# A fused graph, state-space and expert kernel: mask products of the decay exponents replaced by spare contraction rows, and their packets regrouped

## The chip, the cores and the metric

The kernel runs on one core of a Trainium2 chip. The metric is the device time of one execution, in microseconds (us): the median of three timed runs before the change is 3523.06 us (3521.47 to 3528.71). The profile is of one further execution of 3495.61 us.

The engines are TensorE (PE, its weight loads PEld), VectorE (DVE), ScalarE (ACT), GpSimd (POOL) and SyncE (SP). Each has its own instruction stream; they are tied by semaphores.

## The reference, cut to what matters

64 graphs of 256 tokens and 256 features pass through attention over the graph's edges, a state-space block, a product with four kinds of relation, and experts. The change is in the state-space block:

```
dt    = softplus(dt + dt_bias);  A = -exp(A_log)        # 8 heads
dA    = dt * A;  cs = cumsum(dA)                        # per head, over 256 tokens
L     = exp(where(l >= s, cs[l] - cs[s], -inf))         # 8 x 256 x 256
xdt   = x * dt
Y     = einsum('ln,sn,hls,shp->lhp', C, B, L, xdt)      # state size 64, head size 64
```

After it come `Y + x*D`, a product with `silu(z)`, a norm and the output product. Attention (`softmax`, then `probabilities @ wh`) and the relation products belong to other graphs at the same moment, as told below.

## The kernel before, in words

**Steps.** The 64 graphs go through a software pipeline written out by hand. `step(b1_, b2_, b3_, turn_)` issues, on each engine, stage 1 (attention) of graph b1, stage 2 (state space) of graph b2 = b1 - 1 and stage 3 (relations, the row for the experts) of graph b3 = b1 - 2. `rounds` calls it 66 times: some steps written out, and a hardware loop of 28 rounds with two steps each. The order in each engine's stream is the order in the text; nothing reorders it. The two steps of a round differ: one makes the routing decisions of four token tiles (`best_expert`, `counts`; TensorE's small products L1197 to L1202) and is called the routing step here, the other turns them into slots (`slots`, VectorE's L907 to L918) and is called the slot step. The expert stage (71 tiles) follows after all steps.

**The exponents.** Per head the matrix `cs[l] - cs[s]` is made on TensorE in one PSUM bank: 256 columns for sources s in the first 128 tokens and 128 columns for those in the second. `cs3` holds `cs` in bf16 as three parts (high, middle, low), 8 heads each, in 24 rows; four copies of it lie at partitions 0, 32, 64 and 96. `expo(heads, b)` issues a packet: for each of its heads a mask product (L1219, identity times `negmask`, 256 columns, which puts -1e30 above the diagonal), then the products with `sel` (L1224, +cs[l]) and with `selneg` (L1229, -cs[s]), which contract over 24 rows at 32 times q, q = head mod 4. Before, there are two packets: heads 0 to 3 and heads 4 to 7. `EXPO` names the bank of q.

**The chain around them.** `g` is B C^T (in bank 5, with dt turned beside it); ScalarE copies it out (L728 of the listing, L630 in the profile, since the helper `copy` records it). VectorE makes `xdt` (L991). ScalarE takes the exponential of each head (L743) into `decay`, VectorE multiplies pairs of heads by `g` (`weigh`, L868), and TensorE makes Y (L1391). Between these lie, on TensorE: `relate` (L1191, the relation products), the turns of the attention probabilities (L1348), which ScalarE copies out as `probT` (L630), the product with `wh` (L1373), and `attend` (L1184), the next graph's first products. `attend` writes the banks from which VectorE reads for `x1` (L1016), so it waits for `x1_ready`. VectorE's order is: softmax's scores (`nmax`, L975), `xdt`, slots (in the slot step), `weigh` of heads 0 to 3, `x1`, its statistics, `weigh` of heads 4 to 7, y.

## Time and profile before

| | us |
|---|---|
| median of three timed runs | 3523.06 (3521.47 to 3528.71) |
| the profiled execution | 3495.61 |
| its span | 3493.5 |
| TensorE busy | 3387.3 (97%) |
| VectorE busy | 2481.1 (71%) |
| ScalarE busy | 1794.4 (51%) |
| GpSimd busy | 1812.4 (52%) |

The span is the time from the first to the last instruction of the profile; the profiled execution is 2.1 us longer. The busy time of TensorE counts the stretch from a product's start to its modelled end, and neighbouring products overlap, so starts tell more than durations. Where a row of the timeline has xN, its first number is the start of the first of N instructions.

### The profile page before, as it was taken

To read this page: it belongs to the slowest core of one execution; us is meant where nothing else is said; L and a number is where in the kernel's file an instruction comes from. 1 tells how busy PE (TensorE), PEld (TensorE's weight loads), DVE (VectorE), ACT (ScalarE), POOL (GpSimd) and SP (SyncE) were. 2 spreads that over 40 slices of the span, in tenths; PEclk is the share of its full clock that TensorE was granted. 3 is DMA by queue.
4 is the path that set the end of the run, shared out by engine and by line. 5 is a ranking of instruction groups with operands and counts; after the bars stand their busy time and mean duration, and the time that the engine had idled before them with its cause. 6 is when DMAs were issued, how large, how long until landed. Compare 5 with 4: busy or idle time off the path is not lost.

```text
span 3493.5 us, 62587 instructions
## 1 busy us (share of the span) xinstructions
PE 3387.3 (97%) x19338; PEld 2778.6 (80%) x19338; DVE 2481.1 (71%) x7221; ACT 1794.4 (51%) x3818; POOL 1812.4 (52%) x2172
## 2 busy tenths in 40 slices
PE   7999999999999999999999999997799999999998
PEld 6777777777777777777777777775688888888887
DVE  4888888888888888888888888886344444444444
ACT  3655666656656656656666566563232223333322
POOL 3455555555555555555555555554455445555543
PEclk8999999999999999999999999998899999999999
DMA  3111111111111111111111111110455555555553
GB/s 125 40 37 47 44 36 52 39 36 51 39 43 48 36 44 47 36 52 39 36 51 39 42 49 36 45 44 23 161 192 192 197 196 190 194 198 195 194 192 129
DMA packets 168166, 304.67 MB, mean 87 GB/s; under 512 B 38000, under 2 KB 140400, under 8 KB 149936
## 3 DMA queue, kind: packets, MB, share of 16 engines
q0 software_dynamic: 38272, 196.98, 16.4%
q1 hardware_dynamic: 92880, 72.41, 7.3%
q10 hardware_dynamic: 36960, 34.62, 3.4%
q8 instruction: 27, 0.44, 0.1%
q14 instruction: 27, 0.22, 0.0%
HBM read 250.77 MB, written 53.17 MB: 87 GB/s over the span
## 4 chain that ended last, share of the span: by engine, by line
PE 93%; issue 2%; DVE 2%; ACT 1%; another core or an unknown queue 1%; DMA 1%; POOL 0%; SPq 0%; DVEq 0%; ACTq 0%; POOLq 0%
PE bank L1175 15%; PE bank L1447 14%; PE bank L1461 14%; PE bank L1191 13%; PE bank L1292 7%; PE bank L1406 6%; PE bank L1391 5%; PE bank L1184 4%; PE bank L1373 3%; PE bank L1323 2%; PE bank L1245 2%; PE bank L1314 1%; PE bank L1219 1%; PE bank L1413 1%; DVE x L1016 1%
## 5 line engine op out<-in xcount | busy, mean ns | idle before, releaser
L779 ACT ACTIVATE decay<-bank,w_up 128x256 f32<-128x256 f32 x568 | 269.4, 474 | 699.6 <-PE bank L1447 699.6
L1175 PE MATMUL bank<-xn1T,w_in 128*128 128x256 f32 x2304 | 524.9, 382 | 8.0 <-issue 7.2
L1191 PE MATMUL bank<-w_rel,hT 128*128 128x264 f32 x2048 | 523.6, 394 | 0.0
L1447 PE MATMUL bank<-zs,w_up 128*128 128x256 f32 x2272 | 503.9, 380 | 0.6 <-ACT zs L630 0.6
L1461 PE MATMUL bank<-w_dn,decay 128*128 128x256 f32 x2272 | 502.1, 379 | 0.0
L1175 PEld LDWEIGHTS bank<-xn1T,w_in 128*128 128x128 f32 x2304 | 433.2, 190 | 67.0 <-issue 10.4
L1447 PEld LDWEIGHTS bank<-zs,w_up 128*128 128x128 f32 x2272 | 433.0, 191 | 60.1 <-issue 0.9
L1461 PEld LDWEIGHTS bank<-w_dn,decay 128*128 128x128 f32 x2272 | 426.2, 190 | 55.1
L1123 DVE TENSOR_TENSOR hT<-bank,w_dn 128x256 f32<-128x256 f32 x142 | 60.3, 425 | 539.0 <-PE bank L1461 539.0
L859 DVE SCALAR_TENSOR_TENSOR conv<-bank,conv_w,conv 128x255 f32<-128x255 f32 (+2 forms) x960 | 426.2, 477 | 20.9
L1191 PEld LDWEIGHTS bank<-w_rel,hT 128*128 128x128 f32 x2048 | 364.0, 190 | 80.0 <-issue 20.8
L499 POOL TENSOR_SCALAR masks<-adjt_sb 128x512 fp32r<-128x512 int32 x256 | 404.5, 1594 | 5.4
L485 POOL TENSOR_TENSOR rstd<-ve,mhalf 128x2 f32<-128x2 f32 x256 | 217.5, 850 | 279.9 <-DVE ve L844 236.0
L363 POOL TENSOR_TENSOR beats<-mhalf 128x1 f32<-128x1 f32 x372 | 82.4, 221 | 462.1 <-DVE hT L1123 338.7
L868 DVE TENSOR_TENSOR decay<-decay,g 128x768 f32<-128x768 f32 x256 | 251.8, 1025 | 88.7 <-ACT decay L743 86.2
L536 POOL TENSOR_TENSOR x2b<-x,b_rel 128x264 f32<-128x264 f32 x128 | 92.9, 746 | 409.7 <-DVE xdt L991 401.3
L1292 PE MATMUL bank<-masks,xp 128*128 128x512 f32 x1024 | 276.6, 414 | 5.6 <-ACT xp L630 5.6
L743 ACT ACTIVATE decay<-bank 128x384 f32<-128x384 f32 x512 | 209.8, 496 | 115.0 <-PE bank L1229 97.0
L1292 PEld LDWEIGHTS bank<-masks,xp 128*128 128x128 f32 x1024 | 189.5, 190 | 68.5 <-ACT hT L630 25.3
L1406 PE MATMUL bank<-w_proj,y 128*128 128x264 f32 x1024 | 239.1, 387 | 0.3 <-DVE y L1032 0.3
L1406 PEld LDWEIGHTS bank<-w_proj,y 128*128 128x128 f32 x1024 | 189.4, 190 | 30.4 <-DVE y L1032 1.4
L635 ACT ACTIVATE conv<-bank,conv_b,conv_w 128x256 f32<-128x256 f32 x320 | 165.7, 558 | 68.3 <-PE bank L1175 68.3
(242 smaller groups left out, 6063.3 us busy)
## 6 DMA issues: line engine op xcount, KB each, us to landing
token_rows<-row SPq DMA_DIRECT2D x64, 266.0 KB, 3.0
xT_sb<-in_xT ACTq DMA_DIRECT2D x64, 256.0 KB, 2.7
x_sb<-in_x ACTq DMA_DIRECT2D x64, 256.0 KB, 3.0
adj_sb<-in_adj SPq DMA_DIRECT2D x64, 256.0 KB, 3.4
adjt_sb<-in_adjT SPq DMA_DIRECT2D x64, 256.0 KB, 3.4
out<-row SPq DMA_DIRECT2D x64, 256.0 KB, 2.4
w_in<-token_rows,idc POOLq DMA_INDIRECT x142, 4.8
out<-hT,ids POOLq DMA_INDIRECT x142, 2.5
```

Of the source, the lines that this page charges most:

```text
L485: gp.tensor_tensor(rstd[i][:], ve[i][:], mhalf[:], ALU.pow).then_inc(rstd_ready[i], 1)
L499: ins = gp.tensor_scalar(masks[:, :, r, :], adjt[:], float(r + 1), None, ALU.is_equal)
L743: nc.scalar.activation(decay[:, h, :], bank[EXPO[h % 4]][:, 0:TRI], ACT.Exp).then_inc(decay_ready, 1)
L779: nc.scalar.activation(hid(f), bank[f % 4][:, 0:GROUP], ACT.Relu, bias=b1[q % 2][:, f:f + 1]).then_inc(hid_ready, 1)
L859: ins = v.scalar_tensor_tensor(conv[:, c, k:N], src[:, 0:N - k], conv_w[:, c, TAPS - 1 - k:TAPS - k], conv[:, c, k:N], ALU.mult, ALU.add)
L868: v.tensor_tensor(decay[:, 2 * j:2 * j + 2, :], decay[:, 2 * j:2 * j + 2, :], g[:, 0:TRI].unsqueeze(1).broadcast_to([P, 2, TRI]), ALU.mult ...
L1175: ins = mm(dst, w_in[:, k, first:first + P], xn1T[:, k, :], start=k == 0, stop=k == DK - 1)
L1191: ins = mm(bank[6 + t][:, 0:GX], hT[:, d, r * N + t * P:r * N + (t + 1) * P], w_rel[:, r, d, :], start=r == 0 and d == 0, stop=r == R - 1 ...
L1292: ins = mm(bank[6 + c][:, :], xp[part][:, t, d * P:(d + 1) * P], masks[:, t, 2 * c:2 * c + 2, :], start=t == 0 and part == 0, stop=t == T ...
L1406: ins = mm(bank[(4, 2)[t]][:, 0:GX], y[:, j, t * P:(t + 1) * P], w_proj[:, j, :], start=j == 0, stop=j == XB - 1)
L1447: ins = mm(bank[f % 4][:, 0:GROUP], w1[i][:, k, f * P:(f + 1) * P], xgT[:, k, :], start=k == 0, stop=k == DK - 1)
L1461: ins = mm(bank[4 + j][:, 0:D], hid(f)[:, j * P:(j + 1) * P], w2[i][:, f, :], start=f == 0, stop=f == FB - 1)
```

## The change

1. **Masks.** The mask products and `identb`, `negmask` are gone. The contraction now takes all 32 rows of a group. The 29 rows that the head does not use carry, in `cs3`, a function of the position that steps from a tiny value to one at one multiple of 4 each, and in `selneg` -2^60 for the sources in question, so that what lies far above the diagonal is masked by the same products. Rows are prepared once, in VectorE's start; `cs` still comes from one scan (its first operand is now `factors`, its start 1.0).
2. **What is left above the diagonal**, within 4 positions, is cut by `causal` (ones and zeros): VectorE multiplies bank 3 by it and writes `g` (in place of ScalarE's copy), and `weigh` takes min(decay, 1) before it multiplies.
3. **Banks.** `EXPO` is (2, 3, 4, 5), `g` is made in bank 3, x is turned in banks 4 and 5. All eight banks are one tensor, so that ScalarE takes the exponentials of two heads in one instruction of 768 elements.
4. **Packets.** There are three: heads 0 and 1 ahead of `relate(1, range(0, 2))`, heads 2 and 3 where heads 0 to 3 were, heads 4 to 7 where they were. ScalarE takes the exponentials of heads 0 and 1 between the probabilities and the copy `probT`.
5. ScalarE's two copies of 8 columns to `x` are one.

TensorE in a written-out step of all three stages, before, from the turns of x (L1323) to `attend`:

```order
L1323 MATMUL bank<-identf,xs 128x128 x8
L1191 MATMUL bank<-w_rel,hT 128x264 x4
L1348 MATMUL bank<-identf,prob 128x128 x4
L1219 MATMUL bank<-negmask,identb 128x2x128 x4
L1224 MATMUL bank<-cs,sel 128x256 x4
L1224 MATMUL bank<-cs,sel 128x128 x4
L1229 MATMUL bank<-selneg,cs 128x256 x4
L1229 MATMUL bank<-selneg,cs 128x128 x4
L1373 MATMUL bank<-wh,probT 128x264 x4
L1219 MATMUL bank<-negmask,identb 128x2x128 x4
L1224 MATMUL bank<-cs,sel 128x256 x4
```

The same place in the changed kernel (`relate` is L1230 there, the turns of the probabilities L1389, the product with `wh` L1414):

```order
L1362 MATMUL bank<-identf,xs 128x128 x8
L1259 MATMUL bank<-cs,sel 128x256 x2
L1263 MATMUL bank<-cs,sel 128x128 x2
L1268 MATMUL bank<-selneg,cs 128x256 x2
L1268 MATMUL bank<-selneg,cs 128x128 x2
L1230 MATMUL bank<-w_rel,hT 128x264 x4
L1389 MATMUL bank<-identf,prob 128x128 x4
L1259 MATMUL bank<-cs,sel 128x256 x2
L1263 MATMUL bank<-cs,sel 128x128 x2
L1268 MATMUL bank<-selneg,cs 128x256 x2
L1268 MATMUL bank<-selneg,cs 128x128 x2
L1414 MATMUL bank<-wh,probT 128x264 x4
```

The rows of the masks are gone, a packet of two heads stands right behind the turns of x, and a packet of two heads, in place of one of four with its masks, stands between the turns of the probabilities and the product that reads `probT`.

VectorE in the same step, before, from the scores to `x1`:

```order
L975 TENSOR_SCALAR nmax<-emax 128x2
L991 TENSOR_TENSOR xdt<-bank,g 128x512 x2
L868 TENSOR_TENSOR decay<-decay,g 128x768 x2
L1002 RECIPROCAL rsum<-esum 128x2
L1016 SCALAR_TENSOR_TENSOR x<-bank,rsum,x_sb 128x264 x2
```

And in the changed kernel:

```order
L1012 TENSOR_SCALAR nmax<-emax 128x2
L1026 TENSOR_TENSOR g<-bank,causal 128x400
L1030 TENSOR_TENSOR xdt<-bank,g 128x512 x2
L904 SCALAR_TENSOR_TENSOR decay<-decay,g 128x768 x2
L1041 RECIPROCAL rsum<-esum 128x2
L1055 SCALAR_TENSOR_TENSOR x<-bank,rsum,x_sb 128x264 x2
```

The product that makes `g` is new in VectorE's stream, between the scores and `xdt`.

The diff, cut to its core:

```diff
-    EXPO = (2, 5, 3, 4)
+    EXPO = (2, 3, 4, 5)
...
+            def exponentials(j, b):
+                act.wait_ge(expo_made, 8 * b + 2 * j + 2)
+                if j == 0:
+                    need(act, y_made, 2 * b)
+                nc.scalar.activation(decay[:, 2 * j:2 * j + 2, :], expo_banks[j % 2][:, :, 0:TRI],
+                                     ACT.Exp).then_inc(decay_ready, 1)
...
                 nc.scalar.preload_act_table(ACT.Exp)
-                if b2_ is not None:
-                    act.wait_ge(g_made, b2_ + 1)
-                    need(act, m_ready, 4 * b2_)
-                    copy(g[:], bank[5][:, 0:TRI + T * H]).then_inc(g_ready, 1)
...
+                if b2_ is not None:
+                    exponentials(0, b2_)
+                if b1_ is not None:
                     act.wait_ge(prob_turned, b1_ + 1)
                     need(act, hp_made, b1_)
                     copy(probT[:], bank[0][:, :]).then_inc(probT_ready, 1)
                 if b2_ is not None:
-                    for h in range(H):
...
+                    for j in range(1, H // 2):
+                        exponentials(j, b2_)
...
                 for j in pairs:
-                    dve.wait_ge(decay_ready, 8 * b + 2 * j + 2)
-                    v.tensor_tensor(decay[:, 2 * j:2 * j + 2, :], decay[:, 2 * j:2 * j + 2, :],
-                                    g[:, 0:TRI].unsqueeze(1).broadcast_to([P, 2, TRI]), ALU.mult).then_inc(m_ready, 1)
+                    dve.wait_ge(decay_ready, 4 * b + j + 1)
+                    v.scalar_tensor_tensor(decay[:, 2 * j:2 * j + 2, :], decay[:, 2 * j:2 * j + 2, :], 1.0,
+                                           g[:, 0:TRI].unsqueeze(1).broadcast_to([P, 2, TRI]), ALU.min,
+                                           ALU.mult).then_inc(m_ready, 1)
...
-                    ch2.link(dve, v.tensor_tensor_scan(cs[:], ones_row[:], dA[:], 0.0, ALU.mult, ALU.add), b2_)
+                    ch2.link(dve, v.tensor_tensor_scan(cs[:], factors[:], dA[:], 1.0, ALU.mult, ALU.add), b2_)
...
                 if b2_ is not None:
+                    dve.wait_ge(g_made, b2_ + 1)
+                    v.tensor_tensor(g[:], bank[3][:, 0:GW], causal[:], ALU.mult).then_inc(g_ready, 1)
                     dve.wait_ge(g_ready, b2_ + 1)
...
-                    else:
-                        pe.wait_ge(decay_ready, 8 * b + h - 3)
-                    mm(bank[EXPO[h % 4]][:, :].rearrange("p (s l) -> p s l", s=T)[:, :, 0:P], identb[:],
-                       negmask[:].unsqueeze(1).broadcast_to([P, T, P]), start=True, stop=True)
+                    elif h % 2 == 0:
+                        pe.wait_ge(decay_ready, 4 * b + h // 2 - 1)
+                    q, u = h % 4, h // 4
+                    mm(bank[EXPO[q]][:, 0:N], sel[32 * q:32 * q + 32, u, :], cs3[32 * q:32 * q + 32, :],
+                       start=True, stop=False, skip_group_check=True)
...
+                if b2_ is not None:
+                    expo(range(0, 2), b2_)
                 if b3_ is not None:
                     if b1_ is not None:
                         pe.wait_ge(z_ready, b1_ + 1)
                     relate(1, range(0, 2))
...
-                    expo(range(0, 4), b2_)
+                    expo(range(2, 4), b2_)
```

In `expo`, head 1 still waits for `g_ready` and heads 2 and 3 for `xdt_ready`, each ahead of its first product. VectorE's start has some 20 more instructions on single columns or rows, and GpSimd's fills `causal` and a list of positions in place of `negmask` and `identb`.

## Rows read from the trace of the kernel before

**Rows 1.** The page: busy time, and the chain that ended last

```profile
PE 3387.3 (97%) x19338; PEld 2778.6 (80%) x19338; DVE 2481.1 (71%) x7221; ACT 1794.4 (51%) x3818; POOL 1812.4 (52%) x2172
PE 93%; issue 2%; DVE 2%; ACT 1%; another core or an unknown queue 1%; DMA 1%; POOL 0%; SPq 0%; DVEq 0%; ACTq 0%; POOLq 0%
```

**Rows 2.** Two steps by windows: busy us (x instructions), granted clock, DMA share, GB/s

```profile
1500.00:1536.60 36.60, 36.60 (x230) 29.14 (x229) 30.64 (x95) 23.21 (x50) 22.60 (x26) 1.00 0.15 43
1536.60:1573.75 37.15, 36.48 (x224) 28.97 (x223) 32.02 (x92) 23.07 (x49) 18.00 (x21) 1.00 0.16 43
```

**Rows 3.** Waits of TensorE: engine, line <- releaser: us, times, longest

```profile
PE bank L1184 <- DVE x L1016: 15.3, 35, 1.1
PE bank L1391 <- ACT decay L743: 9.0, 6, 3.0
```

**Rows 4.** Timeline of TensorE, routing step: start, us, what, out<-in

```profile
1511.65 1.95 PE L1191 MATMUL bank<-w_rel,hT 128*128 128x264 f32 x8
1513.43 0.60 PE L1348 MATMUL bank<-identf,prob 128*128 128x128 f32 x4
1513.87 0.60 PE L1219 MATMUL bank<-negmask,identb 128*128 128x256 bf16 x4
1514.40 0.34 PE L1224 MATMUL bank<-cs,sel 24*128 24x256 bf16 x8
1514.84 2.05 PE L1373 MATMUL bank<-wh,probT 128*128 128x264 f32 x8
1516.73 0.60 PE L1219 MATMUL bank<-negmask,identb 128*128 128x256 bf16 x4
1517.70 1.16 PE L1191 MATMUL bank<-w_rel,hT 128*128 128x264 f32 x4
1518.82 2.09 PE L1184 MATMUL bank<-w_gc,xT_sb 128*128 128x274 f32 x8
```

**Rows 5.** Chain that ended last, routing step: start, us, what

```profile
1514.04 0.44 PE bank L1219 x4
```

**Rows 6.** Timeline of ScalarE and VectorE, routing step

```profile
1514.07 0.60 ACT L630 ACTIVATE probT<-bank 128x512 f32<-128x512 f32 x1 [1.02 <-PE bank L1348]
...
1511.04 0.17 DVE L975 TENSOR_SCALAR nmax<-emax 128x2 f32<-128x2 f32 x1
...
1515.84 1.83 DVE L868 TENSOR_TENSOR decay<-decay,g 128x768 f32<-128x768 f32 x2 [2.35 <-ACT decay L743]
```

**Rows 7.** VectorE by form: busy, mean ns

```profile
L991 DVE TENSOR_TENSOR xdt<-bank,g 128x512 f32<-128x512 f32 x128 | 82.5, 686 | 48.7 <-ACT g L630 46.8 <-PE bank L1323 1.8
L1123 DVE TENSOR_TENSOR hT<-bank,w_dn 128x256 f32<-128x256 f32 x142 | 60.3, 425 | 539.0 <-PE bank L1461 539.0
L967 DVE SCALAR_TENSOR_TENSOR z<-z 128x256 f32<-128x256 f32 x128 | 48.5, 420 | 7.7 <-ACT z L716 7.0
```

**Rows 8.** Timeline of VectorE, slot step

```profile
1548.05 0.17 DVE L975 TENSOR_SCALAR nmax<-emax 128x2 f32<-128x2 f32 x1
1548.71 1.29 DVE L991 TENSOR_TENSOR xdt<-bank,g 128x512 f32<-128x512 f32 x2 [0.49 <-ACT g L630]
1552.44 2.27 DVE L868 TENSOR_TENSOR decay<-decay,g 128x768 f32<-128x768 f32 x2
1554.82 0.89 DVE L1016 SCALAR_TENSOR_TENSOR x<-bank,rsum,x_sb 128x264 f32<-128x264 f32 x2
```

**Rows 9.** Timeline of TensorE, slot step

```profile
1548.25 1.95 PE L1191 MATMUL bank<-w_rel,hT 128*128 128x264 f32 x8
...
1554.30 1.16 PE L1191 MATMUL bank<-w_rel,hT 128*128 128x264 f32 x4
1555.86 2.09 PE L1184 MATMUL bank<-w_gc,xT_sb 128*128 128x274 f32 x8 [0.40 <-DVE x L1016]
```

**Rows 10.** Timeline of the start: VectorE's last setup instruction and its next

```profile
6.77 0.35 DVE L808 TENSOR_SCALAR selneg<-ones_row,mine_neg 128x256 bf16<-128x256 f32 x1
...
10.44 0.24 DVE L812 SCALAR_TENSOR_TENSOR w_gc<-bank,gate_w 128x8 f32<-128x8 f32 x2 [3.32 <-PE bank L1150]
```

More of the change, by code:

```diff
@@ L97, in sem @@
             return ctx.enter_context(nc.semaphore(name))
-        bank = [ctx.enter_context(nc.psum_tensor(f"bank{i}", [P, 512], F32)) for i in range(6)]
-        bank67 = ctx.enter_context(nc.psum_tensor("bank67", [P, 2, 512], F32))
-        bank += [bank67[:, i, :] for i in range(2)]
+        banks = ctx.enter_context(nc.psum_tensor("bank", [P, 8, 512], F32))
+        bank = [banks[:, i, :] for i in range(8)]
         rows_d = nc.dram_tensor("token_rows", [NT, ROW], F32, kind="Internal").ap()
@@ L1038, in step @@
                     need(dve, rows_out, 16 * b3_)
-                    ins = v.tensor_tensor(row[:, :, 0:GX], bank67[:, :, 0:GX], x2b[:], ALU.add)
+                    ins = v.tensor_tensor(row[:, :, 0:GX], banks[:, 6:8, 0:GX], x2b[:], ALU.add)
                     ins.then_inc(x3_ready, 1)
@@ L1216, in expo @@
                         pe.wait_ge(xdt_ready, 2 * b + h - 1)
-                    else:
-                        pe.wait_ge(decay_ready, 8 * b + h - 3)
-                    mm(bank[EXPO[h % 4]][:, :].rearrange("p (s l) -> p s l", s=T)[:, :, 0:P], identb[:],
-                       negmask[:].unsqueeze(1).broadcast_to([P, T, P]), start=True, stop=True)
+                    elif h % 2 == 0:
[3 more added lines that the diff above has]
+                       start=True, stop=False, skip_group_check=True)
+                for h in heads:
+                    q, u = h % 4, h // 4
+                    mm(bank[EXPO[q]][:, N:TRI], sel[32 * q:32 * q + 32, u, :], cs3[32 * q:32 * q + 32, P:N],
+                       start=False, stop=False, skip_group_check=True)
                 for first, width, s, l in ((0, N, 0, 0), (N, TRI - N, P, P)):
@@ L1223, in expo @@
                         q, u = h % 4, h // 4
-                        mm(bank[EXPO[q]][:, first:first + width], sel[32 * q:32 * q + 3 * H, u, :],
-                           cs3[32 * q:32 * q + 3 * H, l:N], start=False, stop=False, skip_group_check=True)
-                for first, width, s, l in ((0, N, 0, 0), (N, TRI - N, P, P)):
-                    for h in heads:
-                        q, u = h % 4, h // 4
-                        ins = mm(bank[EXPO[q]][:, first:first + width], cs3[32 * q:32 * q + 3 * H, s:s + P],
-                                 selneg[32 * q:32 * q + 3 * H, u, 0:width], start=False, stop=True,
+                        ins = mm(bank[EXPO[q]][:, first:first + width], cs3[32 * q:32 * q + 32, s:s + P],
+                                 selneg[32 * q:32 * q + 32, u, 0:width], start=False, stop=True,
                                  skip_group_check=True)
@@ L1313, in step @@
                     pe.wait_ge(bc_ready, b2_ + 1)
-                    mm(bank[5][:, 0:N], bT[:, 0:P], cT[:], start=True, stop=True)
-                    mm(bank[5][:, N:TRI], bT[:, P:N], cT[:, P:N], start=True, stop=True)
+                    mm(bank[3][:, 0:N], bT[:, 0:P], cT[:], start=True, stop=True)
+                    mm(bank[3][:, N:TRI], bT[:, P:N], cT[:, P:N], start=True, stop=True)
                     for t in range(T):
-                        ins = turn(bank[5][:, TRI + t * H:TRI + (t + 1) * H], dt[0:H, t * P:(t + 1) * P],
+                        ins = turn(bank[3][:, TRI + t * H:TRI + (t + 1) * H], dt[0:H, t * P:(t + 1) * P],
                                    identf[0:H, 0:H])
```

79 lines of the change are left out of this document (54 added, 25 removed).

## The prediction

> **What bounds the kernel now.** I read the page first. TensorE is busy for 97% of the span and holds 93% of the chain that ended last [rows 1], so in general time goes when TensorE's stream gets shorter. The windows of two neighbouring steps come next [rows 2]: the routing step takes 36.60 us and TensorE is busy through all of it; the slot step takes 37.15 us with TensorE busy for 36.48, while VectorE is busy for 32.02. The list of TensorE's waits names the one that recurs in the loop: `attend` (L1184) waits for VectorE's `x1` (L1016), 15.3 us in 35 waits, 0.44 each, about one per pair of steps [rows 3]. The timelines place it. In the slot step `relate` starts at 1554.30 and four products at 0.22 (1.78 us for eight, 1511.65 to 1513.43 [rows 4]) end their issue at 1555.29 or so, behind a packet 0.11 later (below); `attend` starts at 1555.86, right behind `x1`, which ends at 1555.71 [rows 8, 9]. So TensorE is short of work there for 0.45 us by the row, up to 0.55 by starts. VectorE has no pause between `xdt` and `x1` [rows 8]: the half of the loop that ends in `x1` of the slot step is bound by VectorE, the other half by TensorE. In the routing step `relate` starts at 1517.70 and `attend` at 1518.82: 0.11 + 0.89 would give 1518.70, so 0.12 is lost, and its first weight load, no longer hidden, makes it about 0.2. A saving on TensorE therefore counts only in the routing step; in the slot step VectorE decides.
>
> **The change, part by part.**
>
> *Mask products.* Eight per graph, four of them 0.44 us on the chain [rows 5]: 0.88 us per graph, 56 us over 64 graphs, if nothing took their place.
>
> *Contraction over 32 rows for 24.* Same columns, same count. Priced at nothing; I saw no row in which the rows of a contraction change a start.
>
> *A third packet.* What does a packet cost without masks? Mask products start at 1513.87 and would free TensorE at 1514.31; `sel` starts at 1514.40, 0.09 later; the product behind the packet starts at 1514.84, 0.44 after; and the eight behind it take 1.89 (to 1516.73) instead of 1.78 [rows 4]. Sum 0.09 + 0.44 + 0.11 = 0.64 us. In the 0.44 the four heads run beside each other: 8 + 8 products start within 0.44 us. A packet of two heads has the same sequence of widths (256, 128, 256, 128), so I price it the same. The lower bound is half of the 0.44 and the full 0.20 of the edges, 0.42. Three packets 1.92 against two with masks 2 x (0.44 + 0.64) = 2.16: TensorE's own saving is 0.24 us per graph (0.68 at the lower bound of both small packets).
>
> The Trainium skill, TensorEngine Tiling (Array Packing), Key Properties, says that changing the tiling mode drains TensorE, while tiles of one mode work independently. The 0.09 ahead and 0.11 behind a packet agree with it. By that rule the third packet pays its edges however few heads it has; without it three packets would cost 1.32 us and the saving would be 0.84.
>
> *probT, now less covered.* Between the turns of the probabilities (L1348) and the product that reads `probT` stood 0.44 of masks and a packet. The last turn starts at 1513.43 + 3 x 0.11 = 1513.76; the copy starts at 1514.07, 0.31 later, and takes 0.60 [rows 4, 6]; with 0.07 to reach TensorE (estimate, between `x1`'s end and `attend`: 0.15 at most [rows 8, 9]) the reader can start 0.98 after the last turn. TensorE now arrives 0.11 + 0.09 + 0.44 = 0.64 after it. A wait of about 0.33 us per graph takes the place of a mask group (0.2 to 0.4). ScalarE is not late for it: it waited 1.02 us before the copy [rows 6], the `g` copy ahead is gone, and one exponential of 768 elements fits.
>
> *g on VectorE.* A product of 400 elements with one operand in PSUM: 256 take 425 ns, 512 take 686 [rows 7], so 0.57. It can't start before `nmax` ends. Routing step: 1511.21 + 0.03 + 0.57 = 1511.81, at TensorE 1511.88; head 1, which waits for it, could have started at 1511.65 + 0.09: wait 0.13. Slot step: 1548.22 + 0.60 = 1548.82, at TensorE 1548.88 against 1548.25 + 0.09: wait 0.54. `xdt` follows at 1548.85 where it started at 1548.71 (it was waiting for ScalarE's copy) [rows 8]: VectorE's path grows by 0.14, not 0.57. Behind `g` are queued `xdt`, slots, `weigh`, `x1`, and `attend` waits for the last.
>
> *weigh with a min.* The scalar form on 256 elements takes 420 ns, the two-tensor form 425 [rows 7]: same price. In the slot step two weighings take 2.27 us where they take 1.83 in the routing step [rows 6, 8]: 0.44 us is lost beside GpSimd's work. Whether the new form or a start 0.14 later loses this, keeps it or doubles it is not in the trace: -0.44 to +0.44. I take 0, since GpSimd's work there starts when `xdt` is ready and moves along.
>
> The Trainium skill, GPSIMD Engine Reference, Specifications, says that GpSimd shares SBUF interfaces with VectorE and that instructions with two SBUF inputs contend. Both forms of `weigh` have two; by that rule the 0.44 stays, which is what I take.
>
> *Heads 0 and 1 early, ScalarE in pairs.* This starts the exponentials before `relate` and so removes the 0.2 of the routing step; after it the next thing late is TensorE itself.
>
> *Start and end.* VectorE's longer setup has 3.32 us of idle time ahead of L812 to hide in [rows 10]; GpSimd fills one large tile for two small ones. 0, up to +1. At the written-out steps with few fillers TensorE waits for exponentials up to 3.0 us, 9.0 in 6 waits [rows 3]; part of that is shortened: -3 (0 to -5).
>
> **The sum.** From L1191 to `attend`, routing step, before: 1.78 + 0.44 + 0.44 + 0.64 + 1.78 + 0.44 + 0.64 + 0.89 + 0.2 = 7.25. After: 0.13 + 0.64 + 1.78 + 0.44 + 0.64 + 0.33 + 1.78 + 0.64 + 0.89 = 7.27. That is +0.02. Slot step: TensorE's path 1548.25 + 0.54 + 7.14 = 1555.93, no earlier than today's 1555.86; VectorE's path ends 0.14 later and decides: +0.14. A pair of steps costs +0.16, 31 pairs +5; with -3 at the ends +2. Against the profiled execution: 3495.6 + 2 = 3498. The median of the timed runs lies 27.5 us above the profiled execution, for a reason that the trace doesn't show; I put the same +2 on it: 3525 us.
>
> **Rivals.**
>
> *Cheaper packets and a free VectorE (faster).* If small packets cost 0.42 each, TensorE saves 0.44 more per graph, but the wait for `probT` takes 0.22 of it back: routing step 0.02 - 0.22 = -0.20, slot step still +0.14, pair -0.06, with the ends -5: 3518, within the noise. If VectorE also loses no 0.44 beside GpSimd, the slot step falls to TensorE's path, 1555.93 - 0.22 = 1555.71 against 1555.86, -0.15; pair -0.35, 31 pairs -11, ends -3: 3509. A `probT` that isn't waited for gives alone 31 x (0.02 - 0.33 + 0.14) = -5, with the ends -8: 3515. For them: nothing measured two heads alone, and the 0.44 beside GpSimd hangs on which instruction meets which. Against: `sel`'s and `selneg`'s products of four heads already run beside each other, so that columns and not heads make the 0.44 of a packet.
>
> *VectorE's path grows (slower).* In the slot step VectorE already decides, and each 0.1 us there costs 3.1 us. If the 0.44 beside GpSimd comes a second time in the first four heads' weighing, or the new `g` product pays it, the pair is at +0.16 + 0.44 = +0.60, 31 pairs +19, ends -3: 3539. It decides from the first 0.01 us beyond today's end of `x1`. For it: eight small and large VectorE instructions in that stretch vary with GpSimd, the 2.27 among them. Against it: `g` comes before GpSimd's burst.
>
> *All of the removed work counts.* 56 us of masks less 41 of third packets (0.64 x 64): -15, and 31 x 0.2 of waits: -21, 3502. Against it: it needs both new waits to vanish and VectorE to have slack in the slot step, which rows 8 and 9 deny.
>
> **Chances.** A difference below 0.2% (7 us) can't be told from none here. Forecast, within 7 us of 3523: 0.44. Cheaper packets and a free VectorE, or no wait for `probT`, 3509 to 3515: 0.24; everything counts, 3502: 0.05; together faster 0.29. VectorE's path, 3539: 0.27 slower. The range for 8 in 10 takes in 3509 and 3539 and the bounds around them: 3507 to 3542.
>
> **What would show it.** In the changed profile: a packet's edges and body (0.09 ahead, 0.11 behind, 0.44 for two heads as for four); a wait of the product with `wh` for `probT` of some 0.3 us per graph, and of the second head's `sel` for `g`, longer in the slot step; `g` at 0.57 us; no more wait for `x1` in the routing step, a similar one in the slot step; the loop's pair of steps at 73.75 + 0.16 us. I am wrong if a packet of two heads takes 0.2 to 0.3 us, if `probT` is not waited for, or if the weighings in the slot step take 1.83 or 2.7 us.

## The result, and the profile after

| | us, median (range) | ratio to before (95%) |
|---|---|---|
| before | 3524.77 (3521.47 to 3528.71) | |
| changed | 3484.72 (3481.60 to 3485.92) | 0.9885 (0.9867 to 0.9902) |
| predicted | 3525 (3507 to 3542) | |

The changed kernel is 40 us (1.15%) faster than the kernel before, where +2 was forecast. The two profiled executions differ by much less: 3495.61 before, 3485.92 after. That gap between the two comparisons turns out to be the larger half of the miss. The four timed runs of the kernel before were not profiled.

The changed kernel's page, the lines that answer to [rows 1]:

```profile
PE 3378.3 (97%) x18826; PEld 2758.6 (79%) x18826; DVE 2518.6 (72%) x7305; ACT 1743.2 (50%) x3434; POOL 1814.3 (52%) x2172
PE 76%; DVE 15%; issue 6%; ACT 2%; POOL 1%; DMA 1%; ACTq 0%; another core or an unknown queue 0%; DVEq 0%; SPq 0%; POOLq 0%
```

TensorE lost only 9 us of busy time (3387.3 to 3378.3), and VectorE now holds 15% of the chain, where it held 2%.

Two neighbouring windows, as long as a routing and a slot step, but not cut at the points of [rows 2]; columns as there:

```profile
1500.14:1536.57 36.43, 36.18 (x222) 28.72 (x221) 31.23 (x98) 22.33 (x44) 20.19 (x23) 1.00 0.15 44
1536.57:1573.53 36.96, 36.52 (x217) 28.64 (x216) 32.51 (x92) 22.34 (x43) 20.32 (x24) 1.00 0.16 43
```

A step is measured here from the start of one `attend` to the start of the next and named after the step whose `attend` ends it. As medians over the loop the routing step went from 36.72 to 36.43 us, the slot step from 37.03 to 36.95 and the pair from 73.75 to 73.38: -0.36 (unrounded), where +0.16 was forecast. 31 pairs make -11.

TensorE's waits, against [rows 3] (us, times, longest; PEld is the weight load):

```profile
PE bank L1414 <- ACT probT L637: 14.9, 57, 0.7
PEld bank L1259 <- DVE g L1026: 9.3, 29, 0.9
PE bank L1432 <- ACT decay L655: 3.3, 3, 2.2
PE bank L1223 <- DVE x L1055: 1.8, 2, 1.1
```

The new wait for `probT` is there, 0.26 each in these rows; so is the one for `g`, in every second step. The rows count idle time behind the modelled end of a product, so they are shorter than what a wait moves the starts by (below). The wait for `x1` fell from 15.3 to 1.8 us.

TensorE in the routing step, against [rows 4] (L1362 turns of x, L1259 to L1268 a packet, L1230 `relate`, L1389 turns of the probabilities, L1414 product with `wh`, L1223 `attend`):

```profile
1503.18 1.10 PE L1362 MATMUL bank<-identf,xs 128*128 128x128 f32 x8
1504.21 0.28 PE L1259 MATMUL bank<-cs,sel 32*128 32x256 bf16 x2
1504.64 2.05 PE L1230 MATMUL bank<-w_rel,hT 128*128 128x264 f32 x8
1506.53 0.60 PE L1389 MATMUL bank<-identf,prob 128*128 128x128 f32 x4
1507.06 0.28 PE L1259 MATMUL bank<-cs,sel 32*128 32x256 bf16 x2
1507.82 2.05 PE L1414 MATMUL bank<-wh,probT 128*128 128x264 f32 x8 [0.25 <-ACT probT L637]
1509.80 0.29 PE L1259 MATMUL bank<-cs,sel 32*128 32x256 bf16 x4
1510.23 1.16 PE L1230 MATMUL bank<-w_rel,hT 128*128 128x264 f32 x4
1511.23 2.01 PE L1223 MATMUL bank<-w_gc,xT_sb 128*128 128x274 f32 x8
```

A packet of two heads takes 0.43 (1504.21 to 1504.64), one of four 0.43 (1509.80 to 1510.23): the same, as forecast. The eight products behind one take 1.89, so the 0.11 of its far edge is there as well. The product with `wh` starts at 1507.82, where a packet of 0.43 would have let it start at 1507.49: by starts the wait for `probT` costs 0.33.

VectorE and then TensorE in the slot step, against [rows 8, 9]:

```profile
1540.36 0.17 DVE L1012 TENSOR_SCALAR nmax<-emax 128x2 f32<-128x2 f32 x1
1540.43 0.57 DVE L1026 TENSOR_TENSOR g<-bank,causal 128x400 f32<-128x400 f32 x1
1541.04 1.29 DVE L1030 TENSOR_TENSOR xdt<-bank,g 128x512 f32<-128x512 f32 x2
1544.76 2.28 DVE L904 SCALAR_TENSOR_TENSOR decay<-decay,g 128x768 f32<-128x768 f32 x2
1547.15 0.89 DVE L1055 SCALAR_TENSOR_TENSOR x<-bank,rsum,x_sb 128x264 f32<-128x264 f32 x2
```

```profile
1540.67 0.67 PE L1259 MATMUL bank<-cs,sel 32*128 32x256 bf16 x2
1541.06 0.23 PE L1263 MATMUL bank<-cs,sel 32*128 32x128 bf16 x1
...
1541.49 2.05 PE L1230 MATMUL bank<-w_rel,hT 128*128 128x264 f32 x8
...
1547.08 1.16 PE L1230 MATMUL bank<-w_rel,hT 128*128 128x264 f32 x4
1548.19 2.09 PE L1223 MATMUL bank<-w_gc,xT_sb 128*128 128x274 f32 x8
```

From the start of `nmax` to the end of `x1` VectorE took 7.66 us before and takes 7.68 now. `relate` issues until 1547.08 + 0.11 + 0.89 = 1548.08 and `attend` starts at 1548.19: the two engines arrive within 0.11 us of each other. The packet of two heads takes 0.82 here (1540.67 to `relate`, which starts at 1541.49) where it takes 0.43 in the routing step: by starts the wait for `g` costs 0.39.

Last, the loop's jump back. Behind the products L1413 (now L1454) of the slot step the first product of the next round starts (before, then after):

```profile
1565.73 0.60 PE L1413 MATMUL bank<-ones_row,y2s 128*128 128x1 f32 x4
1566.61 1.13 PE L1175 MATMUL bank<-xn1T,w_in 128*128 128x256 f32 x4 [0.27 <-issue]
```

```profile
1558.06 0.61 PE L1454 MATMUL bank<-ones_row,y2s 128*128 128x1 f32 x4
1558.73 1.10 PE L1214 MATMUL bank<-xn1T,w_in 128*128 128x256 f32 x4
```

0.88 us became 0.67, once per pair: 0.21 that no term of the forecast had.

### The profile page after: what moved, and what is told of

Its sections match the earlier page's. It is cut to its first block, busy times and chain, and to the rows that moved or that the text cites. A ratio compares the mean times of both kernels' runs of the same rounds, so it can differ in the third digit from the quotient of the medians.

```text
span 3484.2 us, 60814 instructions
## 1 busy us (share of the span) xinstructions
PE 3378.3 (97%) x18826; PEld 2758.6 (79%) x18826; DVE 2518.6 (72%) x7305; ACT 1743.2 (50%) x3434; POOL 1814.3 (52%) x2172
## 4 chain that ended last, share of the span: by engine, by line
PE 76%; DVE 15%; issue 6%; ACT 2%; POOL 1%; DMA 1%; ACTq 0%; another core or an unknown queue 0%; DVEq 0%; SPq 0%; POOLq 0%
PE bank L1488 14%; PE bank L1502 14%; PE bank L1230 11%; PE bank L1214 8%; PE bank L1432 5%; PE bank L1331 4%; DVE conv L895 4%; PE bank L1414 4%; PE bank L1223 4%; PE bank L1447 4%; DVE stats L875 2%; PE bank L1362 1%; ACT probT L637 1%; PE bank L1477 1%; PE bank L1284 1%
## 5 line engine op out<-in xcount | busy, mean ns | idle before, releaser
L1230 PE MATMUL bank<-w_rel,hT 128*128 128x264 f32 x2048 | 530.0, 397 | 0.0
L1230 PEld LDWEIGHTS bank<-w_rel,hT 128*128 128x128 f32 x2048 | 363.4, 189 | 89.8 <-issue 30.6
L506 POOL TENSOR_SCALAR masks<-adjt_sb 128x512 fp32r<-128x512 int32 x256 | 381.1, 1502 | 5.4
L543 POOL TENSOR_TENSOR x2b<-x,b_rel 128x264 f32<-128x264 f32 x128 | 114.9, 918 | 397.4 <-DVE xdt L1030 389.4
L904 DVE SCALAR_TENSOR_TENSOR decay<-decay,g 128x768 f32<-128x768 f32 x256 | 256.2, 1030 | 68.5 <-ACT decay L655 65.0
L655 ACT ACTIVATE decay<-bank 128x768 f32<-128x768 f32 x256 | 199.4, 805 | 137.4 <-PE bank L1268 131.9
L591 POOL DMA_INDIRECT w_in<-token_rows,idc x142 | 178.8, 1259 | 43.6 <-issue 43.6
```

Of the source, the lines that this page charges most:

```text
L506: ins = gp.tensor_scalar(masks[:, :, r, :], adjt[:], float(r + 1), None, ALU.is_equal)
L655: nc.scalar.activation(decay[:, 2 * j:2 * j + 2, :], expo_banks[j % 2][:, :, 0:TRI], ACT.Exp).then_inc(decay_ready, 1)
L904: v.scalar_tensor_tensor(decay[:, 2 * j:2 * j + 2, :], decay[:, 2 * j:2 * j + 2, :], 1.0, g[:, 0:TRI].unsqueeze(1).broadcast_to([P, 2, TRI ...
L1230: ins = mm(bank[6 + t][:, 0:GX], hT[:, d, r * N + t * P:r * N + (t + 1) * P], w_rel[:, r, d, :], start=r == 0 and d == 0, stop=r == R - 1 ...
```

## The experiments

The runs were made in five sets on four chips: e1 to e4 and e5 to e8 on chip A, e9 to e12 on B, e13 to e16 on C, e17 and e18 on D. The kernel before was timed beside each set. "Pauses" are what is left of a loop when every step is given the usual length of its kind. Medians in us:

| run | kernel | chip | this | before | ratio (95%) |
|---|---|---|---|---|---|
| e1 | before, unaltered | A | 3526.69 | 3528.32 | 0.9997 (0.9988 to 1.0006) |
| e2 | two packets | A | 3505.86 | 3528.32 | 0.9931 (0.9917 to 0.9945) |
| e3 | no min | A | 3520.07 | 3528.32 | 0.9967 (0.9955 to 0.9979) |
| e4 | `relate` split | A | 3498.39 | 3528.32 | 0.9907 (0.9894 to 0.9920) |
| e5 | changed, unaltered | A | 3481.95 | 3517.35 | 0.9909 (0.9894 to 0.9925) |
| e6 | changed, ScalarE shifted | A | 3484.60 | 3517.35 | 0.9909 (0.9894 to 0.9924) |
| e7 | before, ScalarE shifted | A | 3514.34 | 3517.35 | 0.9992 (0.9983 to 1.0001) |
| e8 | masks back | A | 3531.32 | 3517.35 | 1.0043 (1.0029 to 1.0057) |
| e9 | before, no placing | B | 3477.69 | 3501.19 | 0.9940 (0.9925 to 0.9956) |
| e10 | before, one graph | B | 3498.47 | 3501.19 | 0.9991 (0.9981 to 1.0000) |
| e11 | e3 again | B | 3480.71 | 3501.19 | 0.9950 (0.9936 to 0.9963) |
| e12 | split, slots late | B | 3482.43 | 3501.19 | 0.9952 (0.9938 to 0.9966) |
| e13 | changed, unaltered | C | 3500.91 | 3509.20 | 0.9975 (0.9965 to 0.9984) |
| e14 | e3 again | C | 3497.71 | 3509.20 | 0.9966 (0.9953 to 0.9979) |
| e15 | e4 again | C | 3490.66 | 3509.20 | 0.9952 (0.9939 to 0.9965) |
| e16 | e9 again | C | 3476.05 | 3509.20 | 0.9907 (0.9892 to 0.9921) |
| e17 | changed, no placing | D | 3469.84 | 3520.39 | 0.9861 (0.9840 to 0.9881) |
| e18 | before, plain placing | D | 3493.50 | 3520.39 | 0.9927 (0.9906 to 0.9948) |

Pauses in steps 6 to 61 of each profile, added up in us: e1 30, e2 23, e3 42, e4 32; e5 3, e6 4, e7 16, e8 13; e10 3, e11 1, e12 1; e13 21, e14 18, e15 24; none in e9, e16, e17 and e18. The profile ahead of the prediction has 9, the changed kernel's first 4.

e9, e16 and e17 leave the token numbers out of their slots and e18 writes them elsewhere, so the experts work on the numbers of unused slots; e10 works on graph 0 alone. Only their loops are to be read. In e9, e16 and e17 the part behind the last `attend` takes 1149 to 1153 us, against 1162 to 1169 in all others, so some 13 us of their lower times have nothing to do with the loop.

### The kernel before again (e1)

> The kernel before, unchanged, timed against itself with a profile on the same chip as the others here. The changed kernel was timed 40 us (1.15%) faster, but its profiled span is only 9.3 us shorter (3484.2 against 3493.5), of which the loop's regular pairs of steps give 0.36 x 31 = 11. Theory A (stalls of the kernel before that the one profile had few of): timed 3520 to 3530 again, the profile of this run about as long, and in it more irregular pairs of steps than the four of 1.5 to 4.3 us seen before, adding up to about 27 us; the regular pairs are 73.75 us. Theory B (a chip or a day): timed about 3496, so that the change is worth about 10 us. Theory C (a slower steady state): every pair of steps is longer, about 74.6 us.

Theory A holds. Its undisturbed pair is 73.76, yet its profiled execution is 26 us longer than the one shown ahead of the prediction. Of the 26, 22 are pauses in steps 2 to 62, 3 lie in the loads ahead of them and 1 behind. Here is a pause, from 784 us on (ScalarE, TensorE, VectorE; in brackets the idle time before and its releaser, "remote" being none that is known):

```profile
792.85 1.64 ACT L743 ACTIVATE decay<-bank 128x384 f32<-128x384 f32 x4 [9.45 <-remote]
792.52 0.60 PE L1191 MATMUL bank<-w_rel,hT 128*128 128x264 f32 x1 [7.07 <-issue]
792.75 0.89 DVE L1016 SCALAR_TENSOR_TENSOR x<-bank,rsum,x_sb 128x264 f32<-128x264 f32 x2 [8.18 <-issue]
```

By windows, busy us of PE, PEld, DVE, ACT, POOL, then granted clock, DMA share, GB/s:

```profile
786.00:788.00 2.00, 0.00 (x0) 0.00 (x0) 0.00 (x0) 0.00 (x0) 1.29 (x1) 0.79 0.00 0
788.00:790.00 2.00, 0.00 (x0) 0.00 (x0) 0.00 (x0) 0.00 (x0) 0.00 (x0) 0.50 0.00 0
```

TensorE stops ahead of the last of `relate`'s four products, which waits for nothing. What names the pauses in a profile is ScalarE's wait behind the first exponentials, here of this kernel:

```profile
ACT decay L743 <- remote: 41.2, 8, 9.4
```

In the execution ahead of the prediction that line reads 18.0 us, 4 times; in the changed kernel's 5.5, once. The row counts more than the step loses, since ScalarE has slack. So the profiled execution that I worked from was one with few pauses, and the 27.5 us that I set aside as "not shown" were, by e1's profile, for the most part more of them.

### Parts of the change (e2, e3, e4, e8)

e2 puts the packets back as they were, without masks:

```
-                if b2_ is not None:
-                    expo(range(0, 2), b2_)
...
-                    expo(range(2, 4), b2_)
+                    expo(range(0, 4), b2_)
```

> The changed kernel with its packets as before: heads 0 to 3 in one packet between the turns of the probabilities and the product with wh, heads 4 to 7 as they are; ScalarE takes all exponentials (in pairs of heads) behind the copy probT. Masks stay gone. By the record's prices a pair loses 2 x 0.64 of TensorE's third packets, keeps the wait for probT (0.25 seen) and gets the wait for x1 of the routing step back (0.2, more now, since 0.44 of masks no longer covers it). Theory of the record: the early packet is worth little, this kernel is within 5 us of the changed one, either way: TensorE's path to attend is 0.64 shorter, but x1 comes later. Rival (the early packet is what gained): x1 becomes the bound in both steps, the routing step is longer by 0.3 to 0.5 us than the changed kernel's 36.43, and the time is 10 to 20 us above it.

The routing step fell to 36.17, 0.26 under the changed kernel's, and the slot step rose to 37.05; pair 73.22.

```profile
PE bank L1221 <- DVE x L1053: 41.8, 58, 6.4
PE bank L1410 <- ACT probT L637: 14.2, 58, 0.2
```

The wait for `probT` is what it was. In the routing step TensorE saves the third packet, 0.63, and waits for `x1` again, which takes 0.33 of it back (the jump takes 0.05 more); in the slot step the wait for `x1` takes back all of it. So the regrouping into three packets loses 0.16 per pair (73.38 against 73.22), and the gain of the changed kernel comes from elsewhere: from the masks (e8) and the jump. The time, 3505.86, is not to be set beside e5's, since its loop had 23 us of pauses.

e3 makes `weigh` a plain product again (the min, a guard against infinities above the diagonal, is left out):

```
-                    v.scalar_tensor_tensor(decay[...], decay[...], 1.0, g[...], ALU.min, ALU.mult)
+                    v.tensor_tensor(decay[...], decay[...], g[...], ALU.mult)
```

> The changed kernel with weigh as a two-tensor product again, leaving out min(decay, 1), so values above the diagonal are not clipped. The record priced the two forms the same and left open whether the 0.44 us that two weighings lose beside GpSimd in the slot step depends on the form. Theory (form is free): the two weighings of the slot step take as long as in the changed kernel, the pair of steps stays at 73.38, time within 3 us. Rival (the scalar form avoids or adds the loss): weighings in the slot step differ by 0.4 us and the pair of steps by 0.1 to 0.4, 3 to 12 us in all.

Pair 73.44, against 73.38 to 73.42 in the profiles of the changed kernel, and two weighings of the slot step take 2.28 us in either form: the form is free, as forecast. Its 3520 came with 42 us of pauses in the profile.

e4 moves one relation of the second tile behind the packet of heads 2 and 3:

```
-                    relate(1, range(0, 2))
+                    relate(1, range(0, 1))
...
                     expo(range(2, 4), b2_)
+                if b3_ is not None:
+                    relate(1, range(1, 2))
```

> The changed kernel with one of the two relations ahead of the turns of the probabilities (0.89 us on TensorE) moved behind the packet of heads 2 and 3, in front of the product that reads probT, so that it covers the wait for probT (0.25 us by the row in each step, 0.33 forecast). Theory (the wait for probT is a loss in TensorE-bound steps only): the wait is gone, the routing step shortens by 0.25 to 0.3, the slot step by 0.1 or nothing since it waits for x1 instead; 8 to 12 us faster than the changed kernel. Rival (what bounds is ScalarE's and VectorE's chain to x1, and TensorE's wait only moves): the wait turns up at attend, 0 to 3 us.

The wait for `probT` went, and the routing step with it to 36.11, -0.32, which is the 0.33 by starts. The slot step stayed at 36.99, now with a wait for `x1`: VectorE bounds it, and nothing TensorE saves there counts. The time, 3498.39, has 32 us of pauses in it.

```profile
PE bank L1223 <- DVE x L1055: 26.3, 32, 6.3
```

e8 puts the mask products back into the three packets:

```
+                    mm(bank[EXPO[q]]..., identb[:], negmask[:]..., start=True, stop=True)
```

> The changed kernel with its eight mask products of 256 bf16 columns put back into the packets (two in the first, two in the second, four in the third); everything else of the change stays. This undoes the one part that takes columns off TensorE. By the prediction's terms the masks were 0.88 us a graph: the routing step rises from 36.43 to 37.1 to 37.3, the slot step, bounded by VectorE's path, by 0.1 to 0.9; the pair from 73.4 to 74.2 to 75.2, above the 73.75 of before, so 25 to 55 us over e5. Rival (TensorE's removed columns were hidden): pair 73.4 to 73.6 and within 6 us of e5.

Routing step 37.02, slot step 37.50: pair 74.51, +1.1. Eight masks at 0.11 are 0.88, and they cost 0.59 in the routing step and 0.55 in the slot step. In both, two of them (0.22) cover part of the wait for `probT`. The rest, 0.08 and 0.11, is time that TensorE spent on its late `x1` in the slot step (0.11 ahead of `attend`, 0.08 between it and Y). The masks don't cover the wait for `g`: head 1's stands behind it. The changed kernel keeps 1.1 us per pair of the masks' 1.76. The time is 49 us over e5's; 31 pairs make 35 of it, and the profile has 10 us more of pauses.

### Are the pauses the kernel's? (e5, e6, e7, e11, e13, e14)

> The changed kernel, nothing altered. Its span was 3484.2 us with one pause of over 3 us in the loop, while the kernels next to it (e2 to e4) had four to seven such pauses, some 20 to 35 us in all. Theory A (the pauses belong to a run or a chip and fall on every kernel alike): with the kernel before on the same chip at 3523 to 3528, this one now comes to 3505 to 3520, and its profile shows four or more pauses; of the gain only 11 to 20 us are the change's. Theory B (the pauses depend on the kernel's exact instruction stream): it stays at 3480 to 3488 with at most two pauses, and the 28 us beyond the regular steps are real and repeatable for this kernel. Regular pair of steps 73.4 us in both.

3481.95 with two small pauses, on the chip where e2 to e4 had many. That spoke for the exact kernel. The next two move ScalarE's code by 16 tiny instructions ahead of the loop:

```
+                        for k in range(16):
+                            nc.scalar.activation(scratch[:, k:k + 1], a_log[:], ACT.Exp)
```

> The changed kernel with 16 tiny ScalarE instructions (128x1 exponentials into a scratch tile) added once, in the first graph's step, ahead of the loop. They move ScalarE's whole loop by 16 instructions and cost at most 4 us once. Theory B1 (the pauses come from where ScalarE's instructions lie, its instruction stream being read late at one place of the loop): the number of pauses changes against e5, by four or more, time up to 3500 to 3520. Theory B2 (they depend on the loop's timing alone): the loop is the same as e5's, so 3484 to 3490 if e5 has few, and as many as e5 has if it has many. Theory A: as e5 on the same chip, within 4 us.

> The kernel before with the same 16 tiny ScalarE instructions ahead of its loop. Theory B1 (place of the instructions): the pauses move to another step or vanish; the profile's loop then goes from 2339 to about 2315 us and the time from 3526 to about 3500. Theories A and B2: 3524 to 3532, the pauses stay just ahead of ScalarE's second set of exponentials.

e6 is e5 over again, and e7 within 3 us of before, its pauses still ahead of the second set of exponentials (steps 7, 18, 20, 33): a shift of ScalarE's instructions changes nothing, so where they lie is not the cause, as far as one shift can tell.

> The kernel of e3 again, unaltered (the changed kernel with its weighing product as a plain tensor_tensor). In e3 its regular pair was 73.4 us like the changed kernel's 73.4, but 46 us of pauses against 7 made it 3520. Theory K (the pauses go with the exact kernel and repeat): again 40 us or more of them, a time 30 to 38 us over the changed kernel's (3482 to 3485 on this chip). Rival (they belong to the hour: in the first call the kernel before stood at 3528, in the second at 3517): now 3485 to 3500.

The same program as e3 lost its pauses on chip B: 3480.71, 40 us less than on A.

> The changed kernel, unaltered, beside e14 on the same chip. Theory K (pauses go with the exact kernel): if the chip is one that shows pauses (kernel before over 3510), this one still has under 10 us of them and stands at 3480 to 3488 while e14 stands 30 us above. Theory C (chip and hour alone): both show the same pauses, within 5 us of each other in time. On a chip without pauses (kernel before near 3501) both come to 3478 to 3485 and the ratio to before is 0.995, which makes the change itself worth 17 to 20 us.

> The kernel of e3 and e11 (weighing product as a plain tensor_tensor), beside e13. Theory K: 3510 to 3525 where the kernel before is over 3510. Theory C: within 5 us of e13 whatever the chip.

On chip C the changed kernel has pauses too: 7.7, 4.7 and 6.7 us in steps 20, 24 and 30, and e14 has 7.1, 2.4 and 6.2 in the same three. It is within 3.2 us of e14. So few pauses are no fixed property of the changed kernel; the chip and the hour have the larger part in how many a kernel shows, at steps that recur. They are not the whole: in the second set on chip A the changed kernel has 3 and 4 us (e5, e6) and its relatives with masks 16 and 13 (e7, e8). Whether the change itself makes pauses rarer was not told.

### What the pauses follow (e9, e10, e16, e18)

e9 leaves out GpSimd's four indirect DMAs per pair that write token numbers to their slots, and the waits for them:

```
-                g_ = to_place(turn_)
-                if g_ is not None:
-                    place(g_)
```

> The kernel before, with one part left out: GpSimd's indirect DMAs that write the token numbers to their slots (four of 128 rows in every second step, and the waits for them). The experts' stage then works on the numbers of unused slots, so only the loop's profile is read. Theory P (the pauses of the loop, in which ScalarE, and in the long ones TensorE and VectorE too, stand for 4 to 10 us, follow these DMAs, which end 4 to 6 us ahead of them): no pause of over 3 us is left in the loop, and the loop (first to last attention product) takes 2305 to 2315 us against 2327 to 2340 of the kernel before. Rival (the DMAs have no part in it): three to four pauses stay, at step 7 and between steps 18 and 39, 13 to 25 us in all.

> The kernel of e9 (kernel before without the indirect DMAs that place the token numbers), on this chip. Theory P: no pause of over 3 us in the loop even where the kernel before stands over 3510; time 3475 to 3482 on every chip, since it was 3477.7 on the chip without pauses. Rival: pauses as the kernel before has them, 3490 to 3505 where that stands over 3510.

No pause from step 4 on, on chip B, where others had few, and on chip C, where e13 to e15 had 18 to 24 us of them. The order of events on chip C, GpSimd and then ScalarE of e13:

```profile
763.78 0.96 POOL L499 DMA_INDIRECT slot_ids<-tid,slot  x1 [0.30 <-issue]
```

```profile
767.29 0.79 ACT L655 ACTIVATE decay<-bank 128x768 f32<-128x768 f32 x1
769.48 0.60 ACT L637 ACTIVATE probT<-bank 128x512 f32<-128x512 f32 x1 [1.41 <-issue]
777.68 0.81 ACT L655 ACTIVATE decay<-bank 128x768 f32<-128x768 f32 x1 [7.60 <-remote]
```

The last placing DMA is issued 6 us before ScalarE stops. e18 replaces the four by plain DMAs of the same numbers to unused rows:

```
-                    gp.indirect_dma_start(ids_d, bass.IndirectOffsetOnAxis(slot[:, t:t + 1], 0), tid[:, t:t + 1], None)
+                    pool.dma_start(spare_v[g][t], tid[:, t:t + 1])
```

> The kernel before with each of the four indirect placing DMAs replaced by a plain DMA of the same 128 numbers on GpSimd's queue, written to unused rows of the same table (so the experts' stage works on the numbers of unused slots, and only the loop is read). Theory P1 (the indirect form or its scattered addresses make the pauses): no pause of over 3 us on a chip where the kernel before stands over 3505. Theory P2 (any DMA of GpSimd at that place does): the pauses of the kernel before stay, 10 to 30 us of them at steps 20 to 39.

No pause either, on a chip where the kernel before stands at 3520. So the pauses come with the indirect form or with its scattered 4-byte addresses; which of the two was not told. e10 loads graph 0 in every step:

> The kernel before with every step loading graph 0 (features, transposed features and both edge lists), so that all steps work on the same values; the transfers are as large as before. Theory D (the pauses come from the values of some graphs, since they fall on the same steps 7, 19 to 20, 24, 33 and 39 in different kernels): they vanish or fall on every pair of steps alike, pairs all 73.75 or all longer. Rival (time or the program's own course decides): the pauses stay on those steps, 10 to 25 us in all.

It shows 2.1 us at step 7 and 0.9 at step 46 on chip B, where no profiled kernel showed much. It tells nothing on whether values decide.

### The change without pauses (e17)

> The changed kernel without GpSimd's indirect DMAs that write the token numbers to their slots (the same part left out as in e9 and e16). With no pauses in either, the difference to 3476 to 3478 us is the change's own: 31 pairs by 0.36 us are 11, the shorter steps at the loop's start 1 to 3 more: 3461 to 3466 us on any chip. Rival (the change also shortens something outside the regular steps): under 3459.

Steps 2 to 7 and 8 to 62 of e16 (kernel before) and then of e17 (changed), both without placing; length first, then busy us as above:

```profile
76.27:296.70 220.43, 218.12 (x1341) 173.13 (x1341) 181.14 (x524) 139.93 (x294) 107.80 (x125) 1.00 0.13 41
296.70:2324.48 2027.78, 2009.17 (x12373) 1597.73 (x12373) 1719.17 (x5103) 1271.76 (x2668) 999.14 (x1156) 1.00 0.15 43
```

```profile
79.24:297.79 218.55, 216.20 (x1292) 170.85 (x1292) 184.29 (x529) 134.20 (x256) 108.69 (x125) 1.00 0.14 41
297.79:2316.25 2018.46, 1998.77 (x11933) 1576.98 (x11933) 1751.23 (x5158) 1228.08 (x2338) 999.95 (x1156) 1.00 0.15 43
```

2248.21 against 2237.01: the change itself is worth 11.2 us. The timed medians, on different chips, differ by 6 to 8 (3476.05 and 3477.69 to 3469.84); the loads ahead of step 2, which take 72 to 79 us in either kernel, took 3 longer in e17 and explain 3 of the gap. The same two stretches of the kernel ahead of the prediction, of e1, of the changed kernel's first profile and of e13 sum to 2258.6, 2280.4, 2240.7 and 2258.4, so they hold 10, 32, 4 and 21 us of pauses. Of e1 and e13 the long stretch:

```profile
303.56:2355.67 2052.11, 2013.82 (x12372) 1599.77 (x12372) 1722.47 (x5102) 1272.48 (x2668) 1117.02 (x1294) 1.00 0.15 43
```

```profile
296.09:2336.02 2039.93, 2004.33 (x11933) 1580.11 (x11933) 1752.52 (x5158) 1228.39 (x2338) 1115.61 (x1293) 1.00 0.15 43
```

### Two further versions (e12, e15)

e12 adds to e4 that the slots are computed behind the last weighing:

```
-                g_ = to_slot(turn_)
-                if g_ is not None:
-                    slots(g_)
                 if b2_ is not None:
                     weigh(range(0, 2), b2_)
...
                     weigh(range(2, 4), b2_)
+                g_ = to_slot(turn_)
+                if g_ is not None:
+                    slots(g_)
```

> The changed kernel with two moves: relation 1 of the second tile goes from ahead of the probabilities' turns to behind the packet of heads 2 and 3, which covers TensorE's wait for probT (as e4), and VectorE computes the slots behind its last weighing instead of ahead of the first, so that x1 of the slot step is ready 1 us or more earlier. Expected: routing step 36.1 as in e4; slot step from 36.99 down to 36.2 to 36.6, since its end wait for x1 goes; pair 72.3 to 72.7 against 73.4, so 20 to 35 us under the changed kernel, 3450 to 3465, if the pauses stay as few as there; with as many as e4 had, 3470 to 3485. Rival (VectorE's later work, the products with y, is late instead by the slots' time): pair 73.1 to 73.8.

The rival holds: the slot step did fall, to 36.58, but the routing step rose to 36.88, pair 73.47, no better than the changed kernel's. TensorE now waits for y:

```profile
PE bank L1449 <- DVE y L1071: 17.0, 60, 0.5
```

> The kernel of e4 (relation 1 of the second tile behind the packet of heads 2 and 3) beside e13. Its regular pair was 73.10 against 73.39, so 31 pairs give 9 us: 3471 to 3477 where e13 stands at 3482 and neither has pauses. Rival (the pauses fall on it more often than on the changed kernel): 3490 to 3505 on a chip that shows them.

10 us under the changed kernel on the same chip (3490.66 against 3500.91), where 9 were expected, and 18.5 under the kernel before: the fastest of the complete kernels of this set. That the difference is so near 9 is in part luck: the pair accounts for 9 (73.10 against 73.42), but the profiles hold 24 us of pauses against 21, and the two profiled executions are 17 us apart.

## Why the prediction was wrong

Forecast was +2 us and measured -40, and two things make up the 42 between them.

**The base.** The step that failed by most is the one that carried the sum from the profiled execution to the median: "a reason that the trace doesn't show; I put the same +2 on it". It took the 27.5 us for something that stays. They are pauses for the most part: steps 2 to 62 hold 10 us of them in that profile and 32 in e1's (3522.05 us), and only 4 in the profiled run of the result (3485.92 us). 40 us less 11 of the change's own leaves 29, and 32 less 4 is 28. For the timed runs of the result this is inferred, as they have no profile; the loads at the start differ by up to 7 us as well. The trace did show the pauses: `remote` 18.0 us in 4 waits, and four steps of the loop 1.5 to 4.7 us longer than their kind.

**The sum.** Forecast for a pair +0.16, measured -0.36. By the terms:
- Packets, right: 0.43 for two heads as for four, 0.09 ahead and 0.11 behind, so three cost what was said. The Trainium skill (TensorEngine Tiling (Array Packing), Key Properties) has a change of tiling mode drain the engine, and the trace agrees: a packet pays its edge however few heads it has.
- The wait for `probT`, right: 0.33 forecast, 0.33 by starts (0.25 in the row), and e4 wins 0.32 with it.
- The wait of the second head for `g`, mis-sized: 0.54 forecast in the slot step, 0.39 measured by starts; 0.13 forecast in the routing step, none measured. The step that failed is "It can't start before `nmax` ends": `g` starts 0.07 us behind the start of `nmax` (1540.36, 1540.43), 0.10 before its end. From the end of the turns of x to `attend` the routing step takes 7.12 us, forecast 7.27.
- VectorE's path in the slot step, mis-sized by the same error: +0.14 forecast, +0.02 measured (7.66 to 7.68). `xdt` starts 0.68 behind `nmax`, where it started 0.66 behind. The weighings kept their 2.28 with the new form (e3), as taken.
- The 0.2 of the routing step's late `x1`, right: from `relate` to `attend` 1.12 became 1.00, and from `attend` to Y 2.02 became 1.94.
- The loop's jump, in no term: 0.20 per pair in the medians. From product to product it is 0.52 in every variant of the kernel before, 0.32 to 0.35 in the variants with the changed packets and 0.37 in e2 (e12 apart, where these products wait). The masks are not its cause, since e8 has 0.32. What is, stays open.

By position in the pair: from the turns of x to `attend` -0.05 in the routing step and 0.00 in the slot step, from the routing step's `attend` to Y -0.08, the jump -0.20, the rest -0.03; together -0.36. Against the forecast the routing step is 0.15 better, the slot step 0.14, the jump 0.20.

**Start and end.** Forecast -3; steps 2 to 7 gave -1.9 (220.43 to 218.55).

**The rivals.** "Cheaper packets and a free VectorE", priced at 3509, has the right size for the pair (-0.35) by luck: packets are as dear as forecast, and the weighings kept their 2.28. "VectorE's path grows" did not come, with +0.02. The slot step's balance, `x1` and TensorE within 0.11 us, is as close as rows 8 and 9 made it: e4 saves TensorE's wait there and gains nothing, e8 adds 0.88 of masks and pays 0.55.

**Open.** Why the changed kernel met so few pauses in the profiled run of the result, in e5 and in e6, beside kernels with masks that met many, while e13 met 21 us; so whether any of the 29 us is the change's doing. What in the indirect DMAs makes the engines stand; why steps 7, 20, 24, 30, 33 and 39 are the ones; why the jump is shorter. Whether other data moves them was not told by e10.

## What to carry to other kernels

When the profiled execution and the timed median differ by more than the effect that is forecast, look for the difference in the trace first, step by step of the loop, and give the base its own range: here it was worth more than all terms of the change. Where two engines finish a step within 0.1 us of each other, each removed wait uncovers the other engine, so a sum of single terms needs the starts of instructions, not their ends, and not the idle time of the rows either. And a stage can be measured free of a disturbance by leaving out what causes it in both kernels (e16 against e17), which a longer series of timed runs doesn't do.

## What the runs showed of the hardware

- After indirect DMAs that scatter 128 numbers of 4 bytes each, ScalarE, and in the long cases TensorE and VectorE too, stood for 1 to 10 us at some of the steps, with 0.00 DMA share (e1, e13), and while TensorE stood its granted clock fell from 1.00 to 0.50 of full speed. With plain DMAs of the same numbers (e18), or none (e9, e16, e17), no step did so.
- The same program, e3, e11 and e14, took 3520, 3481 and 3498 us on chips A, B and C, for the most part for this reason (42, 1 and 18 us in the profiles); its undisturbed pair was the same within 0.04 us.
- The min and product in one scalar form costs what the plain product costs on fp32 operands (1030 ns for 768 elements against 1032 in e3 and 1025 before).
- A VectorE instruction of 400 columns that did not read the result of the one of 2 columns ahead started 0.07 us after that one's start, while that one lasted 0.17.
